# Spreading VectorE's four weight differences over its queue, and one more unread product on TensorE, in a fused RWKV and mixture-of-experts block

## The reference, cut to what matters

```
h = layernorm(x) * (1 + ca) + sa
x = x + ga * rwkv(h)          # token mix, k/v/r projections, wkv scan over time, output projection
h = layernorm(x) * (1 + cb) + sb
x = x + gb * moe(h)           # 8 experts of 64, top 2, and a shared expert of 128

# inside moe, with x now the rows of h:
logits = x @ gate_w.T
g, u   = x @ Wg[e], x @ Wu[e]           # "gate" and "up", for every expert
y      = sum_e comb[e] * (silu(g) * u) @ Wd[e]
y      = y + silu(x @ sWg) * (x @ sWu) @ sWd
```

## Time and profile before

| | us |
|---|---|
| three runs, median (lowest, highest) | 374.97 (373.86, 377.3) |
| the profiled execution, its own time | 377.31 |
| its span, first to last instruction | 375.5 |
| PE busy (1447 instructions) | 352.0 (94%) |
| DVE busy (617) | 313.5 (83%) |
| ACT busy (439) | 267.9 (71%) |
| POOL busy (75) | 46.4 (12%) |
| mean granted clock of PE | 0.977 |

### The profile page before, as it was taken

The page is one execution under the profiler, slowest core; times in us unless marked ns, Lnnn a source line. Parts: engine busy times, 40 slices in busy tenths (PEclk is TensorE's granted clock), DMA queues, the critical chain, the costliest instruction groups (busy, mean ns, idle before and its releaser), DMA issues.

```text
span 375.5 us, 4537 instructions
## 1 busy us (share of the span) xinstructions
PE 352.0 (94%) x1447; PEld 249.4 (66%) x1447; DVE 313.5 (83%) x617; ACT 267.9 (71%) x439; POOL 46.4 (12%) x75
## 2 busy tenths in 40 slices
PE   4895986899999999999999999999999999989986
PEld 1462543667867776766867677677776686868765
DVE  5987997899999899999889999999799979752541
ACT  3897896958896499849996899759994996141210
POOL 4300063000400230001400140011300100010000
PEclk9997897799999999999999999999999999999999
DMA  8931020000003000500030004000100001000001
GB/s 273 276 111 44 2 98 0 2 1 0 0 3 112 0 3 0 154 2 1 1 114 0 0 2 130 25 0 2 41 16 3 0 0 58 0 0 33 26 0 56
DMA packets 16240, 14.86 MB, mean 40 GB/s; under 512 B 4767, under 2 KB 15193, under 8 KB 16217
## 3 DMA queue, kind: packets, MB, share of 16 engines
q1 hardware_dynamic: 16184, 14.58, 12.8%
q10 hardware_dynamic: 32, 0.01, 0.0%
HBM read 10.38 MB, written 4.21 MB: 39 GB/s over the span
## 4 chain that ended last, share of the span: by engine, by line
PE 84%; ACT 5%; DVE 5%; issue 2%; POOL 2%; DMA 1%; SPq 0%; ACTq 0%; DVEq 0%; POOLq 0%
PE mm L998 31%; PE yo L1029 19%; PE mm L929 18%; PE yo L950 6%; PE tp L849 3%; PE cb L1010 1%; POOL n_rstd L355 1%; PE cb L961 1%; PE cb L963 1%; PE cb L849 1%; DVE n_stats L1306 1%; DMA pool_x<-in_L_wmod_dram 1%; PE mm L1049 1%; PE cb L981 1%; ACT n_xn L380 1%
## 5 line engine op out<-in xcount | busy, mean ns | idle before, releaser
L929 PE MATMUL mm<-mixed,WT 128*128 128x512 f32 x192 | 91.1, 611 | 3.7 <-DVE mixed L1321 3.7
L1029 PE MATMUL yo<-WdG,act 128*128 128x256 f32 x320 | 71.8, 380 | 1.6 <-DVE act L1523 1.6
L1029 PEld LDWEIGHTS yo<-WdG,act 128*128 128x128 f32 x320 | 59.6, 190 | 10.2 <-DVE act L1523 2.7
L929 PEld LDWEIGHTS mm<-mixed,WT 128*128 128x128 f32 x192 | 36.9, 196 | 39.2 <-issue 31.8
L998 PE MATMUL mm<-h_h,w_up_h 128*128 128x512 f32 x160 | 53.5, 416 | 0.0
L998 PE MATMUL mm<-h_l,w_up_h 128*128 128x512 f32 x160 | 50.8, 399 | 0.0
L998 PE MATMUL mm<-h_h,w_up_l 128*128 128x512 f32 x160 | 50.6, 398 | 0.0
L352 POOL TENSOR_TENSOR n_ve<-n_mv,small 128x4 f32<-128x4 f32 x16 | 7.3, 458 | 281.4 <-DVE n_mv L1310 281.4
L511 ACT ACTIVATE pool_g<-mm 128x512 f32<-128x512 f32 x40 | 23.5, 588 | 22.4 <-PE mm L998 22.4
L998 PEld LDWEIGHTS mm<-h_l,w_up_h 128*128 128x128 f32 x160 | 30.5, 191 | 7.5
L998 PEld LDWEIGHTS mm<-h_h,w_up_l 128*128 128x128 f32 x160 | 30.3, 190 | 7.5
(11 more groups left out here) (163 smaller groups left out, 570.0 us busy)
## 6 DMA issues: line engine op xcount, KB each, us to landing
x_in<-in_L_attn_x_dram SPq DMA_DIRECT2D x8, 512.0 KB, 5.0
out_dram<-pool_x SPq DMA_DIRECT2D x5, 512.0 KB, 3.2
gate_rows<-gate_dram SPq DMA_DIRECT2D x4, 384.0 KB, 4.6
pool_x<-in_L_wmod_dram SPq DMA_DIRECT2D x2, 512.0 KB, 6.1
out_dram<-x_third SPq DMA_DIRECT2D x2, 512.0 KB, 3.3
pool_x<-in_L_wmod_dram SPq DMA_DIRECT2D x2, 256.0 KB, 3.9
pool_g<-in_L_ffn_Wg_dram SPq DMA_DIRECT2D x2, 256.0 KB, 5.0
pool_g<-in_L_ffn_Wu_dram SPq DMA_DIRECT2D x2, 256.0 KB, 4.4
```

The lines of the kernel that those rows point to most:

```text
L929: last = nc.tensor.matmul(mm[PROJECT_BANK[c.n][j]][:, :], WT[:, w, kc, oc * P:(oc + 1) * P], mixed[:, w, kc, :], start=(kc == 0), stop=(kc ...
L1029: last = nc.tensor.matmul(dst, act[:, e, t * P:(t + 1) * P], WdG[:, e, :], start=(e == 0), stop=(e == NB - 1))
```

## The change

The function `low_up()`, which made the four differences one after the other between `mix(c1, 2)` and `scan_weight(c1, 1)`, becomes `low_up(gu, kc)`, one difference per call, and the calls are spread: the first stays where all four were, the second follows `scan_weight(c1, 1)`, the third follows `low_part(c0)`, the fourth `offset(c1, 0)`. The order of the four pieces changes too, from row block first to kind first. `up(c0, 0)` now waits for the two pieces of kind 0, and `up(c0, 1)` for all four. PE's list gets one more product that is not read, on bank `yo[1]`, ahead of `turn1(c2, 0)`.

```diff
@@ up(c, i), on PE
                 if i == 0:
                     pe.wait_ge(h2lo_done, c.n + 1)
-                    if c.n == 0:
-                        pe.wait_ge(up_lo_done, 4)
+
+                if c.n == 0 and i < 2:
+                    pe.wait_ge(up_lo_done, KH * (i + 1))
 
                 pe.wait_ge(*UP_AFTER[c.n][i])
@@ PE's list
             project(c1, (4, 5))
+            fill(yo[1], 1)
             turn1(c2, 0)
@@ low_up, on DVE
-            def low_up():
-                for kc in range(KH):
-                    for gu in range(2):
-                        ve.wait_ge(up_hi_done, 2 * kc + gu + 1)
-                        nc.vector.tensor_tensor(w_up_l[:, kc, gu, :], w_up[:, kc, gu, :],
-                                                w_up_h[:, kc, gu, :].bitcast(F32), ALU.subtract
-                                                ).then_inc(up_lo_done, 1)
+            def low_up(gu, kc):
+                ve.wait_ge(up_hi_done, 2 * kc + gu + 1)
+                nc.vector.tensor_tensor(w_up_l[:, kc, gu, :], w_up[:, kc, gu, :],
+                                        w_up_h[:, kc, gu, :].bitcast(F32), ALU.subtract).then_inc(up_lo_done, 1)
@@ DVE's list
             mix(c1, 2)
-            low_up()
+            low_up(0, 0)
             scan_weight(c1, 1)
+            low_up(0, 1)
             low_part(c0)
+            low_up(1, 0)
             offset(c1, 0)
+            low_up(1, 1)
             bias_in(c1)
```

## The result

The changed kernel takes 373.45 us (median of 15 runs, 371.83 to 374.69). The kernel before, run beside it, took 376.55 (15 runs, 373.86 to 377.97). The ratio is 0.9926, with a 95% interval of 0.9907 to 0.9944: 3.1 us between the medians, 0.7%. The profiled execution took 373.97 us with a span of 372.2, against 377.31 and 375.5: 3.3 us less.

What follows compares the result with a forecast made beforehand. TensorE bounds the kernel, held up through ScalarE and GpSimd by VectorE's subtractions, then losing its clock. Its 5.4 us lead shrinks to 3.9, then 3.2 at VectorE's limits: 374.97 - 3.2 = 371.8 us, range 370.0 to 375.2.

Steps and rivals of the forecast that it cites:

- GpSimd is held by the block, and let in by the scan: POOL's power gets in when the first difference gives way to the scan, ending at 56.50; `n_shift` ends 57.62, 2.6 us earlier.
- the 0.94 us of one row: In the kernel before, POOL's power ended 0.94 us after the scan behind the differences started; basis for the predicted entry time.
- ScalarE and the transposes: ACT normalises c2 at 57.9 instead of 60.25, so PE's transposes of c2 can start at 60.03.
- The clock stays up: With PE idle 0.3 us instead of 3.5 ahead of c2's transposes, its clock stays whole; thirty products take 7.05 instead of 8.85.
- PE's lead and VectorE's limit: PE reaches the turn of comb 5.4 us earlier, waits 1.4 us for DVE's route, and its lead falls to 3.9.
- The wait for `tanh_r`: In the ups, the third up waits for ACT's `tanh_r`, moved to 66.85: 0.5 us of stall on PE.
- The second limit: PE waits again, 0.6 us before L1029, for the last `weigh` of c0 ending at 91.81; its lead becomes 3.2 us.
- The total: Whole kernel, 3.2 us gained: 374.1 for the profiled execution, 371.8 for the median.
- my three cases: Outcome against the kernel before, one per cent being 3.75 us: faster 0.33, within 1% 0.60, slower 0.07.
- The rivals: Scan doesn't admit power (0.17, 374.2); clock falls anyway (0.12, 374.2); falls at new wait (0.09, 376.9); larger gain (0.12, 370.5).
- the rival with the new fall: Clock falls at PE's new 1.4 us wait before the turn of comb, from about 1.6 us on; costs 5.1, chance 0.09.
- VectorE beside the power: DVE runs the scan at 55.56 for 1.19 us while the power goes on, then the second difference at 56.75.

Runs made afterwards that it cites:

- e6: The kernel before with the scan moved ahead of the block of four differences, no extra product; 372.98 us, ratio 0.9908.
- e9: The kernel before with the block of four differences moved ahead of the last mixing of c1, a probe; 373.89 us, one run.
- e10: The kernel before with one VectorE memset behind the first of the four differences, the other three bare; 372.11 us, one run.
- e12: The kernel before with one memset between the last mixing of c1 and the block of differences; 373.0 us, ratio 0.9926.
- e2: The kernel before with the extra unread product alone, the four differences still in one block; 375.24 us, ratio 0.997.
- e11: The kernel before with the four differences ordered kind before row block, still one block; 373.87 us, one run.
- e1: The changed kernel without its extra unread product; 373.41 us, ratio 0.9922.
- e5: The kernel before with a one-element addition with two SBUF inputs behind each of the four differences, no extra product; 374.25 us, ratio 0.9943.
- e3: The kernel before with a one-element VectorE memset behind each of the four differences, no extra product; 373.34 us, ratio 0.9934.

## Why the prediction was right, point by point

- **GpSimd is held by the block, and let in by the scan.** Right to the last 0.1 us: 2.13 us against 2.12. `n_shift` ended at 57.71, 57.62 said (57.72 with the 0.10 offset of this execution). But the reason was only half right: a bare border between two differences let a request in that was made while one of them ran (e6, e9, e10, e12; the power took 1.47 us in e9), and shut out one that was made during the mixing ahead of the block (4.33 us in the kernel before, e2 and e11). The prediction had only the 0.94 us of one row to go by, and that the first difference holds the power until the scan came out right without this being known.
- **ScalarE and the transposes.** 57.97 and 60.10 against 57.9 and 60.03.
- **The clock stays up.** It does, and e1 shows that it would without the product. The prediction left open whether a faster run had the fall at all, and put the gain at 1.7 us without it. e11 gives 320.0 - 318.4 = 1.6, and the fall itself 1.8; the timed runs agree, with 375.03 for the kernel before above 0.99 and 373.45 for the changed one. Of the 3.4 us of the profiled pair, about half is the clock's.
- **PE's lead and VectorE's limit.** The ups start at 63.74 (63.52 said). The wait for `tanh_r` was there. PE's wait before the turn of comb was 0.76 us where I had 1.4. This term was mis-sized: the projections of c2 end at 71.48 + 3.59 = 75.07, not at 74.5, because the ups began 0.2 us later than I had it, and the thirty products with their stall, and the projections, took 0.3 us more. It had no effect, since PE waits for VectorE there anyway. The last step of route ended at 75.78 (75.89 said).
- **The second limit.** PE waits for `weigh` at L1030, 0.40 us (0.6 said), and the down products begin at 91.66 against 95.12 less 3.2, 91.9.
- **The total.** 373.97 for the profiled execution against 374.1: the sum was right for the pair that it was worked out for. The median was not: 373.45 lies 1.65 us above my 371.8. The step that failed is taking the 3.2 us, which have the fall of the clock in them, off 374.97. No execution of the kernel before with a mean clock below 0.98 took less than 375.76, so the one at 374.97 most likely had no fall, and for such a one the prediction had its other value, 1.7 us and thus 373.3; measured are 1.6 and 373.45. That the medians of 15 runs lie 3.1 us apart, beside the 3.2 predicted, is in part luck: without the fall the gain is 1.6 us, with it 3.4 by the lengths and 4.0 by the medians (377.45 less 373.45), and the median of the kernel before, 376.55, lies between the two because about two in five of its executions fall. It comes out within 1%, the likeliest of my three cases.
- **The rivals.** The scan did let the power in, and the clock didn't fall at the new waits, nor anywhere behind. The bound of about 1.6 us that I took from a single wait for the rival with the new fall was no bound: 2.66 and 3.52 us (e2, e11) left the clock whole. Its cost of 5.1 us, half of ten microseconds at half clock, was an estimate; the one fall of 10.2 us cost 1.8 us of length (321.8 against the 320.0 of e11).
- **VectorE beside the power.** The scan started at 55.65 and took 1.28 us although the power went on until 56.61, as long as in the kernel before (1.28 us at 57.77), and the second difference began at 56.85 (56.75 said, 56.85 with the offset).

## What to carry to other kernels

When a tiny instruction on GpSimd takes several times what it takes elsewhere, look at what VectorE ran at that moment, and at who waits behind it; here a row of four 128x640 subtractions behind a mixing kept the power, 1.01 us by itself, for 4.33 us, and cutting the row with one small instruction (0.06 us) brought the same as moving the work (lengths of 317.9 and 317.8 in e10 and e12, 318.4 in the changed kernel). Before a wait of TensorE is filled with unread products, see whether the wait itself can be taken away: here the product was then not needed (318.4 with it, 318.4 without it, in e1). And where a stretch gives back more than the next engine can follow, price that engine's queue up to the next join: here the turn of comb could have begun 4.8 us earlier on PE (75.07 against 79.88), and 3.4 us came of it. And where half clock comes in some runs and not in others, take its cost off runs that have it, and not off a median that may not.

## What the runs showed of the hardware that was not expected

- The same wait of TensorE, 3.5 us, was followed by 10.2 us at half clock in one trace and by none in another (e11). Where it falls it costs 1.8 us by the traces, and 29 of 74 runs look like that. A wait of 2.66 us (e2) left the clock whole in the trace, and none of its 12 runs has a mean below 0.98; one of 2.49 us (e9) was followed by 3.4 us at half clock.
- GpSimd's power, 1.01 us by itself, gets in at a border between two VectorE subtractions with two SBUF inputs if it is asked for while one of them runs (e9: 1.47 us). Asked for during the mixing right ahead of the block, it stayed out at four such borders in a row (4.33 us in three kernels). One instruction of 0.06 us ahead of the block lets it in (e12: 1.39 us). The cause of the difference is open.
- A one-element addition with two SBUF inputs opens the way as well as a memset (2.14 against 2.13 us); with four of them the length was 0.4 us more, by one execution each (e5: 318.2, e3: 317.8).
